# Another place in the block for the products around a pipelined attention: hT and q two blocks ahead, layer 0 split over two blocks, x1 in halves

## The reference

```
h = layernorm(x) * (1 + ca) + sa
x = x + ga * attn(h)              # 16 heads of 8 features, output projection, bias
h = layernorm(x) * (1 + cb) + sb
x = x + gb * ffn(h)
```

## Time and profile before

| | us |
|---|---|
| median of 3 runs | 743.62 (743.44 to 745.63) |
| the profiled execution, its own time | 743.44 |
| its span, first to last instruction | 741.6 |
| a block in the middle (blocks 2 to 5) | 80.2 |
| TensorE busy, share of the span | 87% |
| VectorE | 85% |
| ScalarE | 81% |
| GpSimd | 80% |

### The profile page before, as it was taken

The page is one execution under the profiler, slowest core; times in us unless marked ns, Lnnn a source line. Parts: engine busy times, 40 slices in busy tenths (PEclk is TensorE's granted clock), DMA queues, the critical chain, the costliest instruction groups (busy, mean ns, idle before and its releaser), DMA issues.

```text
span 741.6 us, 9757 instructions
## 1 busy us (share of the span) xinstructions
PE 646.9 (87%) x3045; PEld 247.4 (33%) x3045; DVE 632.0 (85%) x778; ACT 598.3 (81%) x555; POOL 596.1 (80%) x404
## 2 busy tenths in 40 slices
PE   5487777877789998999989998999899999987987
PEld 3122222222223343234423352334323443342354
DVE  6789999998999999999999999999999999964110
ACT  2036788986899989998999899998999899979631
POOL 7229698898879998899889997999889887986610
PEclk9556899998999999999999999999999999999999
DMA  4414113241034113422324013411342131001000
GB/s 141 151 58 156 44 51 86 69 147 32 27 91 163 48 48 103 142 75 51 88 68 164 19 42 104 164 50 49 87 141 76 51 90 51 9 9 40 21 19 15
DMA packets 43671, 56.38 MB, mean 76 GB/s; under 512 B 11436, under 2 KB 27076, under 8 KB 43620
## 3 DMA queue, kind: packets, MB, share of 16 engines
q1 hardware_dynamic: 42948, 54.44, 24.2%
q10 hardware_dynamic: 672, 1.31, 0.5%
HBM read 32.06 MB, written 18.89 MB: 69 GB/s over the span
## 4 chain that ended last, share of the span: by engine, by line
PE 45%; DVE 22%; ACT 18%; issue 12%; DMA 1%; ACTq 0%; POOL 0%; DVEq 0%; POOLq 0%
DVE cub L724 10%; PE MB L429 9%; DVE mx L733 9%; PE OP L504 9%; ACT sq L551 7%; PE SA L487 7%; PE Z L472 6%; ACT prob L562 6%; PE MB L439 4%; PE SA L429 2%; ACT hid L605 2%; PE MB L514 2%; PE MB L410 1%; PE MB L411 1%; DVE st L781 1%
## 5 line engine op out<-in xcount | busy, mean ns | idle before, releaser
L850 POOL TENSOR_TENSOR cub<-cub 128x2048 f32<-128x2048 f32 x128 | 460.4, 3601 | 72.9 <-DVE cub L724 71.9
L551 ACT ACTIVATE sq<-Z,shift 128x1024 f32<-128x1024 f32 x256 | 281.8, 1119 | 82.4 <-PE Z L472 81.4
L724 DVE SCALAR_TENSOR_TENSOR cub<-sq,Z 128x1024 f32<-128x1024 f32 x256 | 309.5, 1210 | 27.1 <-ACT sq L551 27.1
L733 DVE TENSOR_REDUCE mx<-SA 128x2 f32<-128x1024 f32 x248 | 301.6, 1216 | 27.2 <-PE SA L487 23.9
L562 ACT ACTIVATE prob<-cub 128x2048 f32<-128x2048 f32 x128 | 245.0, 1916 | 0.0
L487 PE MATMUL SA<-KH,QL 64*128 64x512 f32 x496 | 122.3, 490 | 43.1 <-DVE mx L733 34.7
L472 PE MATMUL Z<-QH,KH 64*128 64x512 f32 x512 | 129.6, 502 | 17.4 <-DVE cub L724 15.5
L504 PE MATMUL OP<-prob,Vq 128*16 128x512 f32 x1024 | 136.6, 608 | 0.4 <-ACT OT L613 0.4
L429 PE MATMUL MB<-hid,W 128*128 128x512 f32 x216 | 119.5, 641 | 0.3 <-ACT hid L605 0.3
L472 PEld LDWEIGHTS Z<-QH,KH 64*128 64x128 f32 x512 | 49.1, 188 | 197.8 <-DVE cub L724 120.1
L487 PEld LDWEIGHTS SA<-KH,QL 64*128 64x128 f32 x496 | 47.9, 190 | 127.3 <-DVE mx L733 97.5
(11 more groups left out here) (126 smaller groups left out, 433.1 us busy)
## 6 DMA issues: line engine op xcount, KB each, us to landing
parts_q<-SQ SPq DMA_DIRECT2D x32, 256.0 KB, 2.5
QL<-parts_q SPq DMA_DIRECT2D x64, 128.0 KB, 2.5
QH<-parts_q SPq DMA_DIRECT2D x64, 128.0 KB, 2.7
KH<-parts_k SPq DMA_DIRECT2D x62, 128.0 KB, 2.6
parts_k<-SK SPq DMA_DIRECT2D x28, 256.0 KB, 2.7
QH<-mp SPq DMA_DIRECT2D x256, 2.0 KB
nd<-OT SPq DMA_DIRECT2D x128, 32.0 KB
xa<-L_attn_x SPq DMA_DIRECT2D x8, 256.0 KB, 3.8
```

Source lines behind the costliest of these rows:

```text
L551: nc.scalar.activation(sq[:, h, :], Z[:, h, :], ACT.Square, bias=shift[:, 0:1]).then_inc(s_sq, 1)
L724: nc.vector.scalar_tensor_tensor(cub[:, m % RING, h, :], sq[:, h, :], CUB_ADD, Z[:, h, :], ALU.add, ALU.mult).then_inc(s_cv, 1)
L733: nc.vector.tensor_reduce(to, unit_bank(m, u)[:, :, :], AX_X, ALU.max).then_inc(s_mx, 1)
L850: nc.gpsimd.tensor_tensor(ff, ff, ff, ALU.mult).then_inc(s_fp, 1)
```

## The change

Three tables are changed, and one helper.

- MISC of the middle blocks: hT and q are made one block earlier (sample b+2 instead of b+1), in steps 11 and 12; v moves from step 13 to 11, h2T from step 13 to 12, y from steps 11 and 12 to 13 and 14; layer 0, which stood in steps 14 and 15, begins in step 15 and ends in steps 0 and 1 of the next block; layer 1 begins in place d of step 1 and its first three tiles end at place c of steps 3, 5 and 7; x1 stands in two halves at places c and d of step 8.
- MISC of blocks -1 and 7 follow: block -1 makes hT and q of sample 1 as well, and block 7 gets two layer-0 products, for which layer 1 moves back; its last tile then has two pieces at each place of step 7. Blocks 8 and 9 are as before.
- FILL: 25 instead of 26 fillers, at other steps.
- AT: `rs2` 11 to 10, `w2g` 8 to 12, `st1` 6 to 4, `mv1` 7 to 5, `rs1` 9 to 8, `xn` 10 to 9.
- `misc_product`: x1 is computed chunk by chunk, with its waits at the first chunk only.

```diff
 MAIN = [
-    ("hT", 1, [(0, "c", 4)]), ("q", 1, [(0, "d", 4)]), ("k", 1, [(1, "c", 4)]),
...
+    ("l0_2", -2, [(0, "c", 4)]), ("k", 1, [(0, "d", 4)]), ("l0_3", -2, [(1, "c", 4)]),
...
-    ("x1", -1, [(8, "c", 4)]),
+    ("x1", -1, [(8, "c", 2), (8, "d", 2)]),
...
-MAIN_AT = {"xbg": 6, "wog": 5, "den_sq": 6, "den_inv": 6, "att": 7, "st2": 9, "mv2": 10, "rs2": 11, "x1n": 11,
-           "w2g": 8, "st1": 6, "mv1": 7, "rs1": 9, "xn": 10}
+MAIN_AT = {"xbg": 6, "wog": 5, "den_sq": 6, "den_inv": 6, "att": 7, "st2": 9, "mv2": 10, "rs2": 10, "x1n": 11,
+           "w2g": 12, "st1": 4, "mv1": 5, "rs1": 8, "xn": 9}
...
             elif name == "x1":
-                pe.wait_ge(s_att, beta + 1)
-                pe.wait_ge(s_wog, beta + 1)
-                pe.wait_ge(s_xbg, beta + 1)
-                for t in range(TB):
+                if first:
+                    pe.wait_ge(s_att, beta + 1)
+                    pe.wait_ge(s_wog, beta + 1)
+                    pe.wait_ge(s_xbg, beta + 1)
+                for t in chunks:
```

More of the change, by code:

```diff
@@ L65 @@
 MAIN = [
[5 rows of a table removed]
[5 rows of a table added]
     ("l1_3", -2, [(9, "c", 1), (9, "d", 1), (10, "c", 1), (10, "d", 1)]),
[4 rows of a table removed]
[3 rows of a table added]
 ]
 MISC = {b: MAIN for b in range(B - 1)}
-MISC[FIRST] = [("hT", 1, [(0, "c", 4)]), ("q", 1, [(0, "d", 4)]), ("k", 1, [(1, "d", 4)]), ("v", 1, [(2, "c", 4)])]
+MISC[FIRST] = [("hT", 1, [(0, "c", 4)]), ("q", 1, [(0, "d", 4)]), ("k", 1, [(1, "d", 4)]), ("v", 1, [(2, "c", 4)]),
+               ("hT", 2, [(11, "d", 4)]), ("q", 2, [(12, "c", 4)])]
 MISC[B - 1] = [
[4 rows of a table removed]
[5 rows of a table added]
     ("x1", -1, [(8, "a", 4)]),
@@ L102 @@
 ]
-FILL = {(FIRST, n): ("v", 1) for n in range(13, 16)}
-FILL |= {(0, n): ("k", 2) for n in range(2, 13)} | {(0, n): ("v", 2) for n in (14, 15)}
-FILL |= {(1, n): ("k", 3) for n in range(2, 8)} | {(1, n): ("x1", 1) for n in range(9, 13)}
-MAIN_AT = {"xbg": 6, "wog": 5, "den_sq": 6, "den_inv": 6, "att": 7, "st2": 9, "mv2": 10, "rs2": 11, "x1n": 11,
-           "w2g": 8, "st1": 6, "mv1": 7, "rs1": 9, "xn": 10}
+FILL = {(FIRST, n): ("q", 2) for n in range(13, 16)}
+FILL |= {(0, n): ("k", 2) for n in range(2, 11)} | {(0, n): ("q", 3) for n in range(13, 16)}
+FILL |= {(1, n): ("k", 3) for n in range(2, 8)} | {(1, n): ("x1", 1) for n in (9, 10)} | {(1, n): ("h2T", 1) for n in (13, 14)}
+MAIN_AT = {"xbg": 6, "wog": 5, "den_sq": 6, "den_inv": 6, "att": 7, "st2": 9, "mv2": 10, "rs2": 10, "x1n": 11,
+           "w2g": 12, "st1": 4, "mv1": 5, "rs1": 8, "xn": 9}
 AT = {b: MAIN_AT for b in range(FIRST, B)}
```

## The result

| | before | changed |
|---|---|---|
| median, same chip | 744.41 us (6 runs, 742.97 to 745.93) | 748.32 us (6 runs, 746.93 to 750.24) |
| the profiled execution | 743.44 | 746.93 |
| its span, mean granted clock | 741.6, 0.961 | 745.1, 0.958 |

The ratio is 1.0056 (1.0038 to 1.0075): slower by half a percent, clear of the noise, and outside the predicted range. The profiled execution of the changed kernel is the fastest of its six; the two profiles differ by 3.5 us where the medians differ by 3.9.

The account below looks back on a forecast made before the run. No engine was full; the bound changed hands among ScalarE, TensorE and VectorE. Blocks 2 to 5 -2.0, block 6 -0.9, block 7 +2.3, block 1 -0.8, block 0 and start -0.7 gave 741.3, stated 741.0; range 735.5 to 747.0 us.

Parts of the forecast that it names:

- the sum's term for block 1: Block 1: x1 gain, thinner step 0 and a loss in steps 11 and 12, together -0.8 us on 82.48.
- the pair: Inputs hT and q, with h2T, in steps 11 and 12: ScalarE late, loss 0.8 us against 1.0 before.
- x1 in halves: Step 8: splitting x1 removes the 0.94 us wait of the maxima behind it, gain 0.9 us a middle block.
- three signs of being wrong: Middle block longer than 80.2 us, y waiting for W2G, or mean clock below 0.80 in blocks 0 and 1.
- The rival that names the clock: Block 0, steps 0 and 1 thinner: clock stays low longer, three steps of +2 us make +6, 747; chance 0.12.
- layers 0 and 1: Steps 15 and 0 to 7: TensorE waits at product changes; cost 0.4 us for layer 0, 0.3 for layer 1.
- denominators: Step 6: ScalarE's two operations on the denominators lose the cover of VectorE's statistics, cost 0.5 us a middle block.
- pair and y: Steps 11 to 14: gain 0.2 us from moving hT, q and h2T, 0.5 from y in steps 13 and 14.
- Rival 2: Bank MB: seven product changes a block instead of four, TensorE waits 0.4 us each; +0.4 a block, 746.4 us; chance 0.17.
- The start's +1.2: Block -1: hT and q between the logits delay the first maxima by 1.2 us, bounds 0 and 3.1.
- Block 7: Extra takes +0.7 us, two more pieces in step 7 ahead of x1 +1.6; together +2.3, bounds +0.7 and +2.8.
- GpSimd: Step 12: W2G ready 1.0 us before y needs it; rival: 1 us late, +7 in seven blocks, 748; chance 0.06.

Follow-up runs that it names:

- more_fill: Changed kernel with a second filler matmul at place d in block 1, step 13's filler moved there: 742.42 us, ratio 0.9984 to the kernel before.
- before_fill: Kernel before with a second filler at place d of steps 2 to 7 and 9 to 12 of block 1: 741.32 us, ratio 0.9962.
- halves_fill: x1_halves with the added block 1 fillers of before_fill: 734.77 us, ratio 0.9867 to the kernel before.
- x1_halves: Kernel before with only x1 split into two halves at places c and d of step 8: 737.03 us, ratio 0.9921.
- l1_whole: more_fill with the first three layer-1 tiles back in whole steps: 738.06 us, ratio 0.9921 to the kernel before.
- no_fill13: Changed kernel without the filler in step 13 of block 1: 747.08 us, ratio 1.0053 to the kernel before.
- late_switch: Changed kernel with blocks -1 and 0 as before; block 1 makes hT, q, k in steps 0 and 1: 746.56 us, ratio 1.0054 to the kernel before.

## Why the prediction was wrong

**The step that failed is the sum's term for block 1.** The prediction had "-0.6 for x1, -1.0 as hT, q are not in step 0 and only half of layer 0 is in it, +0.8 for the pair": -0.8. Measured +3.8. The sum took the clock of block 1 as given. But block 1 isn't at the full clock throughout: its 0.96 was in the rows, and I read it as a matter of block 0. Steps 0 and 1 kept only k of hT, q and k, and two layer-0 products left the block; the clock fell four times instead of twice. more_fill removes all the falls and 7.1 us with them, at the same order. So the +3.8 is made of three: -0.9 for the order, measured at the full clock in both (before_fill 80.1, more_fill 79.2); +7.1 for the falls of the changed kernel; -2.4 for the two falls that before had already. The -0.8 itself was right to 0.1, though not in its items: x1 in halves gives -0.9 (halves_fill 79.2) and all the rest nothing. What it left out, at no price, was the clock. None of the three signs of being wrong appeared either (middle block 80.0, no wait for W2G, mean clocks of 0.85 and 0.90): the sign set for the clock, below 0.80, was too low, as 0.90 in one block was enough.

**The rival that names the clock was right on the mechanism and wrong on the place.** It put the loss in steps 0 and 1 of block 0, thinner by hT and q, with three steps of +2, and a chance of 0.12. Block 0 shows 0.85 in the mean, as before (0.84), and became 0.6 shorter. Its size, 2 us a fall, was good: 1.4 to 2.5 in the steps of the changed kernel, and 1.2 each for the two of before, by the length of the block. Its 747 is near the measured 748.3 by luck, since the place was another. The same argument, less work for TensorE, held for block 1, one block later. (Nor was the stretch before the first rise without gaps, as the rival has it: TensorE waited 1.05 us between hT and q.) The sentence "the trace agrees, with 0.84 in the blocks that fillers pad" lumped blocks 0 and 1 together, where 0.84 is block 0 alone, and 0.96 is a block at the edge.

**The middle block**, -0.5 forecast, -0.2 measured. By the distances of first cubics; x1 is x1_halves against before, the other rows are the changed kernel against x1_halves:

| term | forecast | measured | from |
|---|---|---|---|
| x1 in halves | -0.9 | -0.9 | x1_halves |
| layers 0 and 1 | +0.7 | +0.7 | steps 0 to 6; 0.6 by l1_whole |
| denominators | +0.5 | +0.24 | step 7 |
| pair and y | -0.7 | -0.3 | steps 12 to 14 |

The rows go by steps, and a step can hold two of the moves: steps 0 to 6 also lose hT and q, and step 14 also loses layer 0. Only x1 and, by l1_whole, layer 1 were measured alone. x1 was right, and the waits at the bank were 0.35 four times, near the 0.4 predicted from the earlier trace rows, and once 0.77. Layer 1 was put at +0.3 and costs 0.6; layer 0, put at +0.4, was not tested alone. The denominators were too dear: ScalarE was not late there, it still waited 0.50 for scores at 409.32, just ahead of them. y and the pair together were mis-sized by 0.4: VectorE still waits 0.57 for a square and 0.38 for logits behind steps 13 and 14, so little of y's excess is worked off. Rival 2, the bank, had the waits right and their price wrong: it put the block at +0.4, which is too high by 0.6, and its 746.4 is near the measured median for another reason, by luck.

**The ends.** Block 0 gave 0.6 of 1.9, which settles nothing: it took 80.4 to 82.6 us in the profiles of the old order and 78.3 to 82.6 in those of the new one. The start's +1.2 is met in this profile, and by means it is 0.9, not settled. Block 7 was right where it could be read: steps 0 to 7 are 1.3 longer and step 8 is 0.7 longer, 2.0 against 2.3 forecast. x1's own wait shrank, from 0.90 to 0.35. That the table shows +0.5 comes from 1.5 us at step 10, where the clock fell in the profile of before and not in this one.

**GpSimd** was right: W2G ends 1.4 us ahead of y's first matmul, where 1.0 was worked out; no y waited for it.

**The range** failed with the first step. It reached to 747, where the rivals of +5 and +6 ended, and none of them was combined with the small losses that came true besides, 1.1 in blocks 2 to 5 and 0.4 in block 6.

Open: why the falls stand at steps 3, 6, 9 and 14 and not at others was not settled, nor how much of the two added falls is due to hT and q and how much to layer 0; no_fill13 shows that a fall moves with one filler, and that their number scatters.

## What to carry to other kernels

When a change thins the work of TensorE in a block whose granted clock is not 1.00 throughout, price that as a possible loss (1.2 to 2.5 us a fall here) and test it with fillers before the order is judged. Compare orders with the clock held in both: here that turned +3.8 us of a block into -0.9. Test the parts of a bundle alone: x1 in two pieces carried 0.9 us a block, and the rest cost 0.7. Where products share one PSUM bank, let them change between steps and not within one: for the three tiles of layer 1 it cost 0.6 us a block to do otherwise.

## What the runs showed of the hardware

- In block 1 of the changed kernel the granted clock fell four times to its lower level, with no wait of TensorE above 1.5 us. TensorE stood still for 18.5 us of that block (86.27 less 67.77), in many short waits. With ten fillers more it stood still for 8.1 us (79.20 less 71.10), and the clock stayed at 1.00. On the kernel before, the same addition took it from 17.9 to 8.4 us in waits and from two falls to none.
- A second filler cost nothing at the full clock: steps 2 to 7 of block 1 take 4.54, 4.83, 5.31, 5.06, 4.50 and 6.02 us in late_switch, which lacks it, and 4.52, 4.84, 5.31, 5.06, 4.50 and 6.03 in more_fill. At the lower level a filler took 2.07 and 2.08 us instead of 1.05.
- A low clock need not cost time: in block 0 steps 4 and 5 take 4.52 and 4.78 us without fillers, under the lower level, and 4.52 and 4.79 with two fillers, at the full clock. Steps 0 and 1, which hold hT, q and k, take 5.42 and 6.19 there.
- Executions of one kernel differ, and the clock differs with them: before took 741.68 us at a mean of 0.970, 743.33 at 0.965 and 746.57 at 0.959. A difference of a single profile in blocks 0, 1 and 7 has to be read with the clock beside it.
